# Narrow expert jobs of the first half ahead of the wait for the dispatch, 25 wide and 21 narrow jobs, and result scatters without pauses

## The reference

```
def _L0_ffn_ref(x, w_router, W1, b1, W2, b2, Ws1, bs1, Ws2, bs2):
    D_MODEL, D_FF, N_EXPERTS, TOP_K, N_SHARED = (128, 512, 8, 2, 1)
    SCALE = 1.0 / math.sqrt(N_SHARED + TOP_K / N_EXPERTS)
    probs = jax.nn.softmax(jnp.einsum('btd,ed->bte', x, w_router), axis=-1)
    vals, idx = jax.lax.top_k(probs, TOP_K)
    gates = jnp.sum(jax.nn.one_hot(idx, N_EXPERTS, dtype=x.dtype) * vals[..., None], axis=-2)
    hs = jax.nn.gelu(jnp.einsum('btd,fd->btf', x, Ws1) + bs1)
    acc = jnp.einsum('btf,df->btd', hs, Ws2) + bs2
    h = jax.nn.gelu(jnp.einsum('btd,efd->btef', x, W1) + b1)
    y = jnp.einsum('btef,edf->bted', h, W2) + b2
    acc = acc + jnp.einsum('bted,bte->btd', y, gates)
    return SCALE * acc

x = x + ga * attn(layernorm(x) * (1 + ca) + sa)
x = x + gb * _L0_ffn_ref(layernorm(x) * (1 + cb) + sb, ...)
```

## Time and profile before

| | |
|---|---|
| median of 3 runs | 533.71 us (533.15 to 535.95) |
| the profiled execution's time | 532.91 us |
| its span | 531.1 us |
| granted clock of TensorE, mean | 0.971 |
| TensorE busy | 486.6 us, 92% of the span |
| VectorE, ScalarE, GpSimd busy | 74%, 69%, 66% |
| first job's up, end of the last expert down, end of the span | 349.49, 513.69, 531.1 us |

### The profile page before, as it was taken

How to read it: one execution, slowest core, us unless ns; L and a number is a source line. 1 busy time by engine, 2 the same in 40 slices (tenths; PEclk the granted TensorE clock), 3 DMA queues, 4 the chain that set the end, 5 groups by cost and what they waited for, 6 DMA issues and landing times.

```text
span 531.1 us, 13354 instructions
## 1 busy us (share of the span) xinstructions
PE 486.6 (92%) x4030; PEld 442.3 (83%) x4030; DVE 390.8 (74%) x1613; ACT 365.6 (69%) x1383; POOL 349.4 (66%) x521
## 2 busy tenths in 40 slices
PE   3699999999999999999899979899989999899790
PEld 2489999999999999999747769789979998899680
DVE  4688888888898888988678887427885663343864
ACT  3369999899999999999759588554444544555450
POOL 4257767676776767775320788888888888776640
PEclk9579999999999999999998999999999999999997
DMA  9999900000000000000000114545447788698876
GB/s 194 332 397 393 354 3 1 2 1 3 2 2 2 2 2 2 2 2 2 1 2 0 43 42 134 182 120 172 129 134 217 244 269 260 215 286 265 329 231 184
DMA packets 39277, 68.50 MB, mean 129 GB/s; under 512 B 7475, under 2 KB 25781, under 8 KB 39205
## 3 DMA queue, kind: packets, MB, share of 16 engines
q1 hardware_dynamic: 31764, 56.69, 33.4%
q0 software_dynamic: 4320, 8.99, 4.8%
q10 hardware_dynamic: 3120, 1.97, 1.3%
HBM read 38.16 MB, written 29.46 MB: 127 GB/s over the span
## 4 chain that ended last, share of the span: by engine, by line
PE 62%; POOL 16%; issue 6%; DVE 6%; DMA 5%; ACT 3%; SPq 2%; another core or an unknown queue 1%; POOLq 0%; ACTq 0%; DVEq 0%
PE bank L1418 35%; POOL xs L1287 12%; PE bank L671 8%; PE bank L685 8%; POOL rested L1276 4%; DMA xr<-in_L_attn_x_dram 1%; PE bank L653 1%; DMA xt<-xs 1%; ACT hid L805 1%; DMA yg<-ys 1%; PE bank L566 1%; SPq L217 1%; PE bank L1627 1%; PE bank L1504 1%
## 5 line engine op out<-in xcount | busy, mean ns | idle before, releaser
L1295 POOL DMA_INDIRECT ys<-yo,dst x71 | 71.6, 1008 | 30.9 <-issue 15.2
L1287 POOL DMA_INDIRECT xs<-hrow,slot_i x64 | 62.9, 984 | 38.0 <-issue 38.0
L805 ACT ACTIVATE hid<-bank,slab 128x256 f32<-128x256 f32 (+1 forms) x172 | 62.6, 443 | 29.9 <-PE bank L671 23.0
L685 PE MATMUL bank<-slab,hid 128*128 128x128 f32 x568 | 71.9, 276 | 2.9 <-issue 1.6
L685 PEld LDWEIGHTS bank<-slab,hid 128*128 128x128 f32 x568 | 69.5, 192 | 5.4 <-issue 1.8
L671 PE MATMUL bank<-hg,slab 128*128 128x256 f32 (+1 forms) x344 | 68.8, 343 | 0.5 <-ACT hg L813 0.5
L671 PEld LDWEIGHTS bank<-hg,slab 128*128 128x128 f32 x344 | 55.0, 191 | 5.2 <-issue 0.7
L1174 DVE TENSOR_TENSOR yb<-bank,slab 128x256 f32<-128x256 f32 (+1 forms) x43 | 16.2, 378 | 56.2 <-PE bank L685 32.8
L813 ACT COPY hg<-bank 128x256 f32<-128x256 f32 (+1 forms) x43 | 14.4, 338 | 49.6 <-PE bank L653 34.4
L1276 POOL MEMSET rested<- 128x1408 f32 x32 | 41.3, 1290 | 0.0
L2311 POOL TENSOR_TENSOR nH<-aH,ones 128x128 f32<-128x128 f32 x32 | 14.9, 466 | 33.8 <-ACT aH L1767 33.8
(11 more groups left out here) (423 smaller groups left out, 1809.3 us busy)
## 6 DMA issues: line engine op xcount, KB each, us to landing
slab<-in_slabs_dram SPq DMA_DIRECT2D x43, 578.0 KB
xs<-fill SPq DMA_DIRECT2D x34, 528.0 KB, 7.6
xt<-xs SPq DMA_DIRECT2D x28, 132.0 KB
yg<-ys SPq DMA_DIRECT2D x7, 512.0 KB, 5.8
out_dram<-xr SPq DMA_DIRECT2D x18, 64.0 KB
ys<-yo,dst POOLq DMA_INDIRECT x71
xr<-in_L_attn_x_dram SPq DMA_DIRECT2D x4, 256.0 KB, 6.6
xs<-hrow,slot_i POOLq DMA_INDIRECT x64
```

What stands on the lines that cost most here:

```text
L685: mm = pe.matmul(y[:, s * D:(s + 1) * D], hid[i % 2][:, n, s * P:(s + 1) * P], right, start=(n == 0), stop=(n == FT - 1), skip_group_check ...
L805: nc.scalar.activation(hid[i % 2][:, n, 0:w], e_half(i, n)[:, 0:w], ACT.Gelu_apprx_tanh, bias=bias).then_inc(e_x, 1)
L1287: pool.indirect_dma_start(out=xs[:, :], out_offset=bass.IndirectOffsetOnAxis(ap=slot_i[:, i, c:c + 1], axis=0), in_=hrow[:, c, :], in_offs ...
L1295: pool.indirect_dma_start(out=ys[:, :], out_offset=bass.IndirectOffsetOnAxis(ap=dst[v][:, s:s + 1], axis=0), in_=yo[v][:, s, :], in_offset ...
```

## The change

- `ORDER` goes from `WW.WW.WW.WW.W.` + `WWWW` + 6 `WH` + 2 `WWH` + `WWWWW` + `HHHHHHH` + `..` to `WW.WWWWHWHWHWHH.HH` + `WWW` + 4 `WH` + `.` + 4 `WH` + `WWWWW` + `.` + `HHHHHH` + `...`: 25 wide and 21 narrow jobs, 46 in place of 43 (still 71 units). Ahead of the wait for the second half of the dispatch stand 9 wide, 7 narrow and 2 shared jobs, where 9 wide and 5 shared stood.
- The tables of the 7 early narrow jobs come from new VectorE operations (`early_halves` after the first job's post, `begin_rest` after the second's); SyncE waits for them before the rows of expert job 6.
- GpSimd's pauses among the result scatters are gone; those in the dispatch stay. `RY` is 18.
- SyncE issues all the loads of `ys` after the last slab. The sums move: `SUMS` now names the last five jobs only.
- `hs`, the hidden tiles of the shared MLP, share their buffers with `hid`.

```diff
-N_WHOLE = (2 * B * S // P - E) // 2
+FULL_HALVES = -(-(B * S - E * (P - 1)) // P) - SUB * N_FULL
+N_EARLY = N_FULL + FULL_HALVES
+N_REST = 16
+N_WHOLE = N_FULL + N_REST
-ORDER = "WW.WW.WW.WW.W." + "WWWW" + 6 * "WH" + 2 * "WWH" + "WWWWW" + "HHHHHHH" + ".."
+ORDER = "WW.WWWWHWHWHWHH.HH" + "WWW" + 4 * "WH" + "." + 4 * "WH" + "WWWWW" + "." + "HHHHHH" + "..."
...
-LOAD_AT = BY_HALF + 6
 RX = 4
-RY = 10
-RW = 5
+RY = 18
...
-        hs = [psb(f"hs{i}", [P, FT, SH]) for i in range(2)]
+        hs = hid
...
             sp.wait_ge(s_half[0], 16 * CH)
-            for j in range(N_FULL):
+            for j in range(N_EARLY):
+                if j == EARLY_HALF:
+                    sp.wait_ge(table_ready, 4)
                 rows(j)
                 if j >= RW:
                     weights(j)
-            sp.wait_ge(table_ready, 4)
-            weights(N_FULL)
-            weights(N_FULL + 1)
+            sp.wait_ge(table_ready, 6)
+            weights(N_EARLY)
+            weights(N_EARLY + 1)
             sp.wait_ge(s_half[1], 16 * CH)
-            for j in range(N_FULL, N_TILES):
+            for j in range(N_EARLY, N_TILES):
                 rows(j)
...
-                if j == LOAD_AT:
-                    scattered(sp, BY_HALF)
-                if LOAD_AT <= j < LOAD_AT + 4:
-                    load(sp, j - LOAD_AT)
+            scattered(sp, BY_HALF)
+            for g in range(4):
+                load(sp, g)
...
+            def early_halves():
+                seen = past[:, 0:N, :]
+                then(dve.tensor_reduce(full_by[:, :], over[:, :, :], AX_X, ALU.add))
+                then(dve.tensor_scalar(begun[:, :], marks[:, 0:E], float(SUB), None, ALU.mult))
...
+                dve.tensor_scalar(e_i[:, early], etab[:, early], float(E - 1), None, ALU.min).then_inc(table_ready, 1)
...
+                dve.wait_ge(table_ready, 3)
+                dve.tensor_copy(row_i[:, early], rowf[:, early]).then_inc(table_ready, 1)
...
-            SUMS = {-12: (0, 1), -11: (2, 3), -10: (4, 5), -9: (6,), -8: (7,), -7: (8,), -6: (9,), -5: (10,), -4: (11,), -3: (12, 13, 14, 15), -2: (16,)}
+            SUMS = {-5: (0,), -4: (1, 2, 3, 4, 5), -3: (6, 7, 8, 9, 10, 11), -2: (12, 13, 14, 15, 16, 17)}
...
             for i in range(len(JOBS)):
                 prepare(i + 2)
                 e_post(i)
-                if i == 2:
+                if i == 0:
+                    early_halves()
+                elif i == 1:
+                    begin_rest()
+                elif i == 3:
                     rest_marks()
...
             for j in range(N_TILES):
                 scatter(j)
-                quads = sum(WIDE[:j + 1]) // 4
-                if quads > sum(WIDE[:j]) // 4 and j < N_TILES - 7:
-                    pause(15 + quads)
```

More of the change, by code:

```diff
@@ L34 @@
 N_SH = B * S // SH
+RW = 5
 PARTS = ((0, 2), (2, 4), (4, 6), (6, 8))
@@ L412, in program @@
         held, marks = psb("held", [P, 3, E]), psb("marks", [P, 4 * E])
-        over = psb("over", [P, E, CAP // TS])
+        over = psb("over", [P, E, CAP // P])
         tri = psb("tri", [P, 3 * E, E])
         odd, units, clipped = (psb(n, [P, 3 * E]) for n in ("odd", "units", "clipped"))
+        full_by, begun, left = psb("full_by", [P, E]), psb("begun", [P, E]), psb("left", [P, 3, E])
         run, marksh = psb("run", [P, E]), psb("marksh", [P, 4 * E])
@@ L1027, in counted @@
                                               op0=ALU.mult, op1=ALU.add))
-            wholes_at = cut["step"].rearrange("p (k o) -> p k o", o=2)[:, :, 0]
             def full_tiles():
                 ts = slice(0, N_FULL)
-                seen, grid = past[:, 0:N_FULL, :], [P, E, CAP // TS]
+                seen, grid = past[:, 0:N_FULL, :], [P, E, CAP // P]
                 counted(0)
-                then(dve.scalar_tensor_tensor(out=over[:, 0:E, :], in0=held[:, 0, :].unsqueeze(2).broadcast_to(grid),
-                                              scalar=-float(TS - 1), in1=wholes_at.unsqueeze(1).broadcast_to(grid),
+                then(dve.scalar_tensor_tensor(out=over[:, :, :], in0=held[:, 0, :].unsqueeze(2).broadcast_to(grid),
+                                              scalar=-float(P - 1), in1=cut["step"].unsqueeze(1).broadcast_to(grid),
                                               op0=ALU.add, op1=ALU.is_gt))
-                then(dve.tensor_reduce(full[:, :], over[:, 0:E, :], AX_X, ALU.add))
+                then(dve.tensor_reduce(full[:, :], over[:, :, :].rearrange("p e (k o) -> p e k o", o=2)[:, :, :, 1], AX_X, ALU.add))
                 then(dve.tensor_tensor(tri[:, 0:E, :], full[:, :].unsqueeze(1).broadcast_to([P, E, E]),
@@ L1056, in full_tiles @@
                 then(dve.tensor_tensor(marks[:, 1:E], last[:, 0, 1:E], last[:, 0, 0:E - 1], ALU.subtract))
-            n_rest, V, U = N_WHOLE - N_FULL, 3 * E, CAP // P
-            rest, halves, spare = slice(N_FULL, N_WHOLE), slice(N_WHOLE, N_TILES), xn[:, :, :, :].rearrange("p k c d -> p (k c d)")
+            n_rest, V, U, N = N_REST, 3 * E, CAP // P, FULL_HALVES
+            early, rest, halves = slice(N_WHOLE, N_WHOLE + N), slice(N_FULL, N_WHOLE), slice(N_WHOLE + N, N_TILES)
+            spare = xn[:, :, :, :].rearrange("p k c d -> p (k c d)")
@@ new lines, in begin_rest @@
+            def begin_rest():
+                then(dve.tensor_scalar(last[:, 0, :], last[:, 0, :], float(N), None, ALU.min))
+                then(dve.tensor_tensor(begun[:, 1:E], begun[:, 1:E], last[:, 0, 1:E], ALU.add))
+                then(dve.tensor_tensor(begun[:, 1:E], begun[:, 1:E], last[:, 0, 0:E - 1], ALU.subtract))
+                then(dve.tensor_tensor(begun[:, 0:1], begun[:, 0:1], last[:, 0, 0:1], ALU.add))
+                then(dve.tensor_scalar(marks[:, 0:E], begun[:, :], 1.0 / SUB, None, ALU.mult))
+                then(dve.scalar_tensor_tensor(out=left[:, :, :], in0=begun[:, :].unsqueeze(1).broadcast_to([P, 3, E]), scalar=-float(P),
+                                              in1=held[:, :, :], op0=ALU.mult, op1=ALU.add))
@@ L1071, in rest_marks @@
                 dve.wait_ge(turned, NG)
-                then(dve.tensor_tensor(over_all, held[:, :, :].rearrange("p k e -> p (k e)").unsqueeze(2).broadcast_to(grid),
+                then(dve.tensor_tensor(over_all, left[:, :, :].rearrange("p k e -> p (k e)").unsqueeze(2).broadcast_to(grid),
                                        cut["step"].unsqueeze(1).broadcast_to(grid), ALU.is_gt))
@@ L1078, in rest_marks @@
                                        odd[:, 2 * E:3 * E].unsqueeze(1).broadcast_to([P, 3, E]), ALU.min))
+                then(dve.tensor_tensor(each(marks[:, E:4 * E]), each(marks[:, E:4 * E]),
+                                       marks[:, 0:E].unsqueeze(1).broadcast_to([P, 3, E]), ALU.add))
+                then(dve.tensor_tensor(each(units[:, :]), each(units[:, :]), begun[:, :].unsqueeze(1).broadcast_to([P, 3, E]), ALU.add))
             def ends(at):
@@ L1167, in e_post @@
                     dve.wait_ge(e_yb, i + 1)
-                    if j >= EARLY_SH + 5:
+                    if j >= BIASED:
                         dve.wait_ge(xs_ready, NG)
```

56 lines of the change are left out of this document (37 added, 19 removed).

## The result

The changed kernel takes 551.7 us in the median (550.3 to 553.2, four runs), the kernel before 534.1 beside it: 1.031 times as long, 95% interval 1.027 to 1.034. I had forecast 530.0, and 521 to 542 as the range. It is slower, and outside the range.

A forecast was written before the change was run, and what follows sets the result against it. Expert part taken as TensorE jobs plus 12.0 us of holes. 349.49 + 157.7 - 8.8 + 21.9 = 520.3 us, plus holes of 2.8 + 4.7 + 0.4 = 7.9 and 1.8 outside the span, gave 530.0; range 521 to 542.

The forecast's parts named there:

- (1): Expert part: 25 wide, 21 narrow and 7 shared TensorE jobs take 157.7 us, 0.2 us more than before.
- (7): Kernel's end: last expert result 8.8 us before TensorE's end, then 21.9 us to the span's end, against 17.4 before.
- (3): Early tables: VectorE's added small operations cost 0; without the second result bank's cover, 1 to 4 us once.
- (4): Early narrow jobs, about 375 to 403, beside dispatches in fours: late signals cost 2.8 us, bounds 0 and 6.
- (5): Result scatters without pauses: late signals cost 4.7 us in the late narrow-mixed stage, bounds 0 and 16.
- Rival B: Without pauses, lateness holds at 3.5 us through all 8 late pairs: 16 us lost, not 4.7; 541.3 us, chance 0.24.
- (2): Wait for the dispatch's second half: the 1.81 us hole goes, since rows are wanted later; next late would be a slab.
- (6): Last narrow jobs: loads of summed rows behind the last slab end their queueing; slab 0 to 1.5 us late, taken 0.4.
- Rival A: An unbroken stream of scatters lets signals pass, so nothing is lost to lateness after 393: 523 us, chance 0.20.

The follow-up runs named there:

- e4: The changed kernel with pauses after each four units put back among the result scatters for expert jobs 0 to 25 only: 539.0 us, 1.007 of before.
- e7: e4 with SyncE fetching the second half's first rows ahead of two slabs, and the last two table steps two jobs later: 1.009 of before.
- e14: e7 with a pause after each three units among the result scatters, for expert jobs 0 to 29: 0.992 of before.
- e16: e14 unchanged, measured once more on another chip: 1.003 of before.
- e9: e4 with GpSimd beginning its result scatters only when job 17 is posted: 1.033 of before.
- e2: The kernel before without its pauses among the result scatters, all else as in before: 547.9 us, 1.025 of before.
- e15: The changed kernel unchanged, measured once more on another chip: 1.029 of before.
- e3: The changed kernel with a pause after each eight units among the result scatters: 553.0 us, 1.035 of before.
- e1: The changed kernel with the pauses after each four units put back among the result scatters: 540.9 us, 1.013 of before.
- e8: The kernel before with all loads of summed rows behind the last slab and the sums at the last four jobs and after: 1.005 of before.
- e13: The kernel before with a pause after each three units among the result scatters, not four: 1.005 of before.
- e10: e4 with a quarter of the pause among the result scatters, 352 columns cleared in place of 1408: 1.032 of before.

## Why the prediction was wrong

- **The sum of the jobs (1) and the end (7)** held. From the last expert down (ends 529.5) to the end it is 21.8 us, forecast 21.9. The sum with the measured numbers closes: 354.5 + 157.7 + 26.1 - 8.8 + 21.8 = 551.3, with 26.1 as the time that TensorE lost from first up to last down.
- **(3), the tables,** cost nothing that the traces show. In after VectorE writes the last of the early ones at 366.6, and the fetches of rows and slabs go on from 368.6.
- **(4), the early narrow jobs:** forecast 2.8 (0 to 6), measured 4.0 in after, 1.8 in e4 and 6.6 in e7 (jobs 9 to 14), and 2.7 in e14, without late signals. There two thirds of it is a wait for rows. In range, but the mechanism that I gave is only a part of it.
- **(5), the pauses, is the step that failed.** I priced an unbroken run of some 55 scatters by one of five, since the lateness beside it (2.8 us) was no greater than beside runs of four, and took 4.7, in the late narrow-mixed stage. Measured are 21.8, right behind the dispatch. Where signals are late, the loss grows with the run: 6.1 us beside 9 scatters (e16), 11.2 beside 15 (e9), 15.1 beside 16 (e2), 21.8 beside 19 (after), 24.8 beside 21 (e15), and 20.3 beside two runs of 8 (e3). The lateness isn't a constant that each pair of jobs pays; while the run lasts next to nothing gets through. It ends itself: TensorE starves, makes no more units, GpSimd has scattered all by 418.6 (I had said 465), and its own waits from there on are the pauses. That is why the mixed stage has no hole afterwards.
- **Rival B** had the sign and the mechanism: late signals as long as the backlog lasts. It had neither the place nor the size: its price, 541.3, took 3.5 us of lateness over the 8 pairs of the late narrow-mixed stage, and what came is one hole of 22 us ahead of them, while those pairs lost nothing. Its condition, lateness above 2.9 us, was met at fewer jobs and by far: 11.7 to 19.7.
- **(2), the dispatch wait,** went as a wait for the dispatch, and came back as another, which the pauses' hole hides in after: 6.3 to 6.7 us at jobs 17 to 19 in e1 and e4, against 2.0 in before. I had named the slabs as next late, and not that the rows themselves stand behind a slab. That queueing is worth 2.4 (e9); the rest goes with the scatters. That this stage of four narrow jobs around a shared one bears late signals badly is my reading.
- **(6), the narrow end:** 0.4 forecast, 0.4 measured. The chain of waits of the kernel after has the last slab there:

```profile
520.95 3.84 DMA slab<-in_slabs_dram
```

3.84 us, not the 5.6 to 6.1 of the loads that I took as its bound. But it was issued at 520.95, only 3.6 us before TensorE wanted it, where I had it asked for 4.9 us ahead; TensorE waited 0.2. Two misses cancelled, so the 0.4 is partly luck. The Trainium skill, "DMA: Bandwidth & Descriptors", section "Anatomy of one DMA — SWDGE (gpsimd) path", gives an estimate of 3.4 for these 578 KB by its fit of 2.0 us plus bytes over 436 GB/s; for this transfer, on another kind of queue, the trace is near to it, and for the loads of the earlier trace rows it is not. And e8 shows that the moved loads alone don't make the stage run so well. What else does, the rest of the order or the scatters that are done in time, is not shown.
- So with its pauses the change is still no gain where signals are late (1.007 and 1.013), since in e1 5.6 at the early narrow jobs and 6.3 at jobs 17 to 19 outweigh the 2.0, 2.8 and 4.4 that it saves at the dispatch wait, in the mixed stage and in the last narrow jobs; the jobs and the end add some 1.1. Rival A, no lateness, has its case in e14: 3.0 us of holes, an unbroken run of 23 scatters without a loss, and 0.992 of before, though with e7's and e14's edits. The changed kernel itself has no trace without late signals.

What stays open: by what the indirect DMAs hold TensorE and its signals (instructions, semaphores or something else), why e13 and e14 don't show it, and with it what the changed kernel takes where signals are not late.

## What to carry to other kernels

When an engine's regular pauses are to be removed, look for how long its longest run becomes, and don't price it by the runs that the pauses made; the backlog at the start of the run tells its length (18 to 21 units here, and runs of 16 to 21). A pause that looks like idle time may be what the others live on, and e10 shows that its length matters. Measure such an effect more than once before building on it: two of these traces didn't have it at all. When an order is changed so that a wait is covered, follow also what stands ahead of the awaited transfer in its own queue.
